# Cross-attention with sparsemax and a trigonometric FFN on one core: the context arrives transposed from the host instead of being transposed by TensorE

## What is computed

```
q = layernorm(x) @ Wq + bq;  k = ctx @ Wk + bk;  v = ctx @ Wv + bv      # 16 heads of 32
attn = sparsemax(q k^T / sqrt(32));  x = x + (attn v) @ Wo + bo
z = layernorm(x);  x = x + sqrt((z @ cos(theta+theta_noise))^2 + (z @ sin(phi+phi_noise))^2)
```

## Time and profile before

| | us |
|---|---|
| median of 3 runs | 852.85 |
| the three runs | 851.33, 852.85, 861.3 |
| the profiled execution: its span, first to last instruction (no time of its own beside it is given) | 858.3 |
| busy in it: TensorE matmul / its weight load | 681.9 / 441.6 |
| busy: VectorE / ScalarE / GpSimd | 639.5 / 480.7 / 195.8 |

### The profile page before, as it was taken

How to read it: one execution, slowest core, us unless ns; L and a number is a source line. 1 busy time by engine, 2 the same in 40 slices (tenths; PEclk the granted TensorE clock), 3 DMA queues, 4 the chain that set the end, 5 groups by cost and what they waited for, 6 DMA issues and landing times.

```text
span 858.3 us, 17053 instructions
## 1 busy us (share of the span) xinstructions
PE 681.9 (79%) x5152; PEld 441.6 (51%) x5152; DVE 639.5 (75%) x4046; ACT 480.7 (56%) x936; POOL 195.8 (23%) x147
## 2 busy tenths in 40 slices
PE   3895843879977789899889988988949898986485
PEld 3562522645555454665467455855437455742351
DVE  2799995599936997499929994799638995899401
ACT  3271754655485554875388546765537566843441
POOL 4940450001520034102520162004410053000000
PEclk9898885979989799899989999999969999998687
DMA  7620100000020000200020002000020000000000
GB/s 233 247 99 1 68 3 1 2 2 1 11 90 1 0 10 1 90 0 0 10 91 0 0 10 67 24 0 10 1 86 4 0 10 11 3 1 10 11 3 10
DMA packets 14576, 26.27 MB, mean 31 GB/s; under 512 B 2106, under 2 KB 2106, under 8 KB 14478
## 3 DMA queue, kind: packets, MB, share of 16 engines
q1 hardware_dynamic: 14478, 25.35, 8.9%
HBM read 23.71 MB, written 1.64 MB: 30 GB/s over the span
## 4 chain that ended last, share of the span: by engine, by line
DVE 71%; issue 9%; PE 7%; DMA 5%; DVEq 3%; SPq 3%; ACT 2%; ACTq 0%; POOL 0%; POOLq 0%
DVE cand L772 22%; DVE cand L784 17%; DVE top L779 14%; DMA xq<-in_x 3%; PE tps L438 3%; DVE csum L794 2%; PE work L422 2%; DMA out_y<-att 2%; DVE x L871 2%; DVE gk L797 2%; DVE topz L790 1%; DVE g_max L800 1%; SPq L197 1%; DVE st L747 1%; PE work L342 1%
## 5 line engine op out<-in xcount | busy, mean ns | idle before, releaser
L772 DVE MAX8 cand<-S 100x8 f32<-100x60 f32 (+1 forms) x1536 | 191.0, 208 | 49.0 <-ACT S L576 28.7
L438 PE MATMUL tps<-ident,S 100*128 100x100 f32 x768 | 106.0, 282 | 82.3 <-DVEq L864 47.5
L422 PE MATMUL work<-kT,qz 128*100 128x361 f16 x768 | 153.8, 342 | 0.8 <-ACT k_f L597 0.8
L613 ACT ACTIVATE S<-S,neg_tau 100x722 f32<-100x722 f32 x128 | 115.0, 900 | 68.2 <-DVE neg_tau L802 68.2
L287 POOL TENSOR_TENSOR ctxT<-ctxT_f,ctxT 128x1024 f16<-128x1024 f32 x24 | 54.0, 2248 | 426.5 <-ACT ctxT_f L576 426.5
L784 DVE MATCH_REPLACE8 cand<-top,cand 100x96 f32<-100x96 f32 x640 | 149.1, 250 | 0.0
L337 PE MATMUL work<-wv,ctxT 128*128 128x512 f16 x576 | 130.8, 384 | 19.8 <-ACT v L576 19.4
L779 DVE MAX8 top<-cand 100x8 f32<-100x96 f32 x768 | 141.2, 252 | 0.0
L438 PEld LDWEIGHTS tps<-ident,S 100*128 100x128 f32 x768 | 87.0, 158 | 104.0 <-ACT pT L576 45.5
L337 PE MATMUL work<-ctxT,wk 128*128 128x361 f16 x768 | 128.3, 329 | 10.8 <-ACT k_f L597 9.1
L576 ACT ACTIVATE S<-work 100x722 f32<-100x722 f32 x128 | 99.6, 778 | 33.0 <-PE work L422 30.8
(11 more groups left out here) (102 smaller groups left out, 671.4 us busy)
## 6 DMA issues: line engine op xcount, KB each, us to landing
ctx_nat<-in_ctx SPq DMA_DIRECT2D x8, 1280.0 KB
xq<-in_x SPq DMA_DIRECT2D x8, 200.0 KB
xr<-in_x SPq DMA_DIRECT2D x8, 200.0 KB
out_y<-att SPq DMA_DIRECT2D x8, 200.0 KB
ctx_nat<-in_ctx SPq DMA_DIRECT2D x8, 164.0 KB
wq<-in_L_xattn_Wq SPq DMA_DIRECT2D x1, 1024.0 KB, 7.4
S<-in_L_xattn_Wk SPq DMA_DIRECT2D x1, 1024.0 KB, 9.5
S<-in_L_xattn_Wv SPq DMA_DIRECT2D x1, 1024.0 KB, 11.2
```

What stands on the lines that cost most here:

```text
L422: last = nc.tensor.matmul(buf[0:L, half, 0:HALF], qz2[:, i, h // G, h % G, :], kT2[:, j, h // G, half * HALF:(half + 1) * HALF], start=(n ...
L438: last = nc.tensor.transpose(tps[:, half, c * L:(c + 1) * L], S[0:L, h, kc * P:(kc + 1) * P], ident[0:L, 0:L])
L613: nc.scalar.activation(S[0:L, h, 0:N], S[0:L, h, 0:N], ACT.Relu, bias=neg_tau[:, h:h + 1], accum_out=row_sum[:, h:h + 1]).then_inc(relu_do ...
L772: last = nc.vector.max(cand[:, j, 8 * i:8 * i + 8], S[0:L, h, cuts[i]:cuts[i + 1]])
```

## The change

The host hands the context over as (batch, 128, 4, 722), that is with the model dimension over the partitions, outside the measured time. SP loads it with one transfer straight into `ctxT_f`, now (128, 4, 722) fp32. ScalarE casts it from there to `ctxT2[:, 0]`, one instruction for each i, the third of 210 columns a chunk; GpSimd's `low_ctx` is as before but for the shorter third. `transpose_ctx` and `ctx_nat` are gone. `load_ctx(b+1)` waits for `low_ctx` of batch b. Since the ring's uses in a pass must be even, `q_of` is split in two halves on TensorE and ScalarE (28 uses instead of 30), and the semaphores that guard each slot are chosen anew. `v_of(b, 1)` starts when the slot before v0 is read, no longer when v0 is; `v_of(b, 2)` when v0 is. GpSimd zeroes the pad columns of `ctxT2` instead of the pad rows of `ctx_nat`, and the first load no longer waits for it. The diff, cut to its core:

```diff
 
-    USES = H + 1 + NC // 2 + 1 + 1 + NC // 2 + 1 + DC
+    USES = H + 1 + NC // 2 + 2 + 1 + 1 + DC
 
...
         ctxT2 = sb("ctxT2", [P, 2, DC, NC * P], F16)
-        ctxT_f = sb("ctxT_f", [P, DC, 2 * P])
+        ctxT_f = sb("ctxT_f", [P, DC, N])
         kT2 = sb("kT2", [P, 2, DC, N], F16)
...
@@ -183,12 +182,9 @@
         def _(sp):
             def load_ctx(b):
 
-                sp.wait_ge(ctx_f_ready, NC // 2 * b)
-                src = ctx_in[bass.ds(b, 1), :, :]
-                sp.dma_start(ctx_nat[:, 0:NC - 1, :],
-                             src[:, 0:(NC - 1) * P, :].rearrange("a (c p) d -> p (a c) d", p=P)).then_inc(in_ctx, 16)
-                sp.dma_start(ctx_nat[0:LAST, NC - 1, :],
-                             src[:, (NC - 1) * P:N, :].rearrange("a p d -> p (a d)")).then_inc(in_ctx, 16)
+                sp.wait_ge(ctx_lo_ready, NC // 2 * b)
+                sp.dma_start(ctxT_f[:, :, :],
+                             ctx_in[bass.ds(b, 1), :, :, :].rearrange("a p c n -> p (a c) n")).then_inc(in_ctx, 16)
 
             def load_x(buf, b, done):
                 sp.dma_start(buf[:, :], x[bass.ds(b, 1), :, :].rearrange("a l d -> l (a d)")).then_inc(done, 16)
             load_x(xq, 0, in_xq)
-            sp.wait_ge(pad_zero, 1)
-            load_ctx(0)
+            sp.dma_start(ctxT_f[:, :, :],
...
         def _(pool):
-            pool.memset(ctx_nat[64:P, NC - 1, :], 0.0).then_inc(pad_zero, 1)
+            pool.memset(ctxT2[:, :, :, N:NC * P], 0.0).then_inc(pad_zero, 1)
...
 
-                pool.wait_ge(ctx_f_ready, NC // 2 * b + i + 1)
-                at = slice(2 * i * P, 2 * (i + 1) * P)
-                pool.tensor_tensor(ctxT2[:, 1, :, at], ctxT_f[:, :, :], ctxT2[:, 0, :, at],
+                pool.wait_ge(ctx_hi_ready, NC // 2 * b + i + 1)
+                at = slice(2 * i * P, min(2 * (i + 1) * P, N))
+                pool.tensor_tensor(ctxT2[:, 1, :, at], ctxT_f[:, :, at], ctxT2[:, 0, :, at],
                                    ALU.subtract).then_inc(ctx_lo_ready, 1)
                 pool.wait_ge(ctx_lo_ready, NC // 2 * b + i + 1)
...
@@ TensorE @@
-            def q_of(b, before_v=False):
+            def q_of(b, half, sem_before, value):
...
+                pe.wait_ge(sem_before, value)
                 buf = take()
-                for m in range(DC):
+                for m in (2 * half, 2 * half + 1):
...
-            def transpose_ctx(b, i, att_before=0, v_between=True):
...
-                for j in range(2):
-                    for c in range(DC):
-                        last = nc.tensor.transpose(buf[:, j, c * P:(c + 1) * P],
-                                                   ctx_nat[:, 2 * i + j, c * P:(c + 1) * P], ident[:, :])
-                last.then_inc(work_full, 1)
...
                 if i == 0:
                     pe.wait_ge(s_ready, H * (b + 1))
+                elif i == 1 and last_pass:
+                    pe.wait_ge(att_ready, b)
+                elif i == 1:
+                    pe.wait_ge(xT_ready, b + 2)
                 else:
-                    pe.wait_ge(v_ready, NC // 2 * b + i)
-                    if last_pass:
-                        pe.wait_ge(att_ready, b)
+                    pe.wait_ge(v_ready, NC // 2 * b + i - 1)
...
                 for i in range(NC // 2):
-
                     v_of(b, i, last)
-                    if not last:
-                        transpose_ctx(b + 1, i, None if first else b)
                 if not last:
-                    q_of(b + 1)
+                    q_of(b + 1, 0, v_ready, NC // 2 * b + 2)
+                    q_of(b + 1, 1, v_ready, NC // 2 * b + 3)
...
                     else:
-                        x2T_of(b - 1, ctx_f_ready, NC // 2 * (b + 2))
-                        k_of(b + 1, 0, b)
+                        x2T_of(b - 1, q_raw_ready, 2 * (b + 1) + 1)
+                        k_of(b + 1, 0, q_raw_ready, 2 * (b + 1) + 2)
...
                     if not last:
-                        for m in range(1, DC):
-                            k_of(b + 1, m, b)
+                        k_of(b + 1, 1, k_f_ready, DC * (b + 1) + 1)
+                        k_of(b + 1, 2, sq_ready, b)
+                        k_of(b + 1, 3, k_f_ready, DC * (b + 1) + 2)
@@ ScalarE @@
-            def q_of(b):
-                copy(q_raw[:, :, :], empty()[:, 0, 0:DC * L].rearrange("p (m l) -> p m l", m=DC),
+            def q_of(b, half):
+                ms = slice(2 * half, 2 * half + 2)
+                copy(q_raw[:, ms, :], empty()[:, 0, 2 * half * L:2 * (half + 1) * L].rearrange("p (m l) -> p m l", m=2),
                      scale=SCALE).then_inc(q_raw_ready, 1)
 
             def ctxT_of(b, i):
 
-                src = empty()
-                for part, dst in ((0, ctxT2[:, 0, :, 2 * i * P:2 * (i + 1) * P]), (1, ctxT_f[:, :, :])):
-                    if part == 1 and (i > 0 or not at_start(b)):
-                        act.wait_ge(ctx_lo_ready, NC // 2 * b + i)
-                    for j in range(2):
-                        last = copy(dst[:, :, j * P:(j + 1) * P], src[:, j, :].rearrange("p (c k) -> p c k", c=DC))
-                last.then_inc(ctx_f_ready, 1)
+                if i == 0:
+                    act.wait_ge(in_ctx, 16 * (b + 1))
+                at = slice(2 * i * P, min(2 * (i + 1) * P, N))
+                copy(ctxT2[:, 0, :, at], ctxT_f[:, :, at]).then_inc(ctx_hi_ready, 1)
...
+        if name == "ctx_1024":
+            a = np.asarray(a).reshape(a.shape[0], a.shape[1], -1, P).transpose(0, 3, 2, 1)
```

More of the change, by code:

```diff
@@ L61, in build_kernel @@
     B, L, D = x.shape
-    N = ctx_in.shape[1]
+    N = ctx_in.shape[3]
     H = 16
@@ L90, in build_kernel @@
         wcos, wsin = sb("wcos", [P, DC, D]), sb("wsin", [P, DC, D])
-        ctx_nat = sb("ctx_nat", [P, NC, D])
         ctxT2 = sb("ctxT2", [P, 2, DC, NC * P], F16)
-        ctxT_f = sb("ctxT_f", [P, DC, 2 * P])
+        ctxT_f = sb("ctxT_f", [P, DC, N])
         kT2 = sb("kT2", [P, 2, DC, N], F16)
@@ L148, in build_kernel @@
         weight_step, split_ready = sem("weight_step"), sem("split_ready")
-        ctx_f_ready, k_f_ready, q_sum = sem("ctx_f_ready"), sem("k_f_ready"), sem("q_sum")
+        ctx_hi_ready, k_f_ready, q_sum = sem("ctx_hi_ready"), sem("k_f_ready"), sem("q_sum")
         ctx_lo_ready, k_lo_ready = sem("ctx_lo_ready"), sem("k_lo_ready")
@@ L356, in q_of, with k_of @@
                 last.then_inc(work_full, 1)
[L358 to L379 removed]
+            def k_of(b, m, sem_before, value):
                 if m == 0:
                     pe.wait_ge(ctx_lo_ready, NC // 2 * (b + 1))
[L384 to L389 removed]
+                pe.wait_ge(sem_before, value)
                 buf = take()
@@ L490, in _ @@
             xT_of(0, take()).then_inc(work_full, 1)
-            for i in range(NC // 2):
-                transpose_ctx(0, i, None, False)
             pe.wait_ge(in_wq, 16)
-            q_of(0, True)
+            q_of(0, 0, xT_ready, 1)
+            q_of(0, 1, xT_ready, 1)
             pe.wait_ge(split_ready, 1)
-            for m in range(DC):
-                k_of(0, m)
+            k_of(0, 0, q_raw_ready, 1)
+            k_of(0, 1, q_raw_ready, 2)
+            k_of(0, 2, k_f_ready, 1)
+            k_of(0, 3, k_f_ready, 2)
             pe.wait_ge(split_ready, 2)
@@ L523, in one_pass @@
                     v_of(b, i, last)
-                    if not last:
-                        transpose_ctx(b + 1, i, None if first else b)
                 if not last:
-                    q_of(b + 1)
+                    q_of(b + 1, 0, v_ready, NC // 2 * b + 2)
+                    q_of(b + 1, 1, v_ready, NC // 2 * b + 3)
                 if first:
-                    for m in range(DC):
-                        k_of(b + 1, m)
+                    k_of(b + 1, 0, q_raw_ready, 2 * (b + 1) + 1)
+                    k_of(b + 1, 1, q_raw_ready, 2 * (b + 1) + 2)
+                    k_of(b + 1, 2, k_f_ready, DC * (b + 1) + 1)
+                    k_of(b + 1, 3, k_f_ready, DC * (b + 1) + 2)
                     sum_flags(b, 0)
```

41 lines of the change are left out of this document (11 added, 30 removed).

## The result

| | before | after |
|---|---|---|
| median of 13 runs each, us | 854.18 | 844.62 |
| lowest and highest, us | 849.02, 861.3 | 841.15, 846.76 |
| profiled execution: span / its own time, us | 858.3 / not given | 840.8 / 843.08 |

The ratio is 0.9896, 95% interval 0.9871 to 0.992: 1.0% faster, 9.6 us between the medians. The spread of the runs fell from 12.3 to 5.6 us. The forecast was 847.0 us, within 838 to 855, and a change of under 2%.

A forecast was written before the change was run, and what follows sets the result against it. The chain was taken as 71% VectorE, with TensorE and ScalarE hardly on it. From the median of 852.85 us, 1.4 for x1 and 4.5 for the other terms gave 847.0 us, range 838 to 855.

The forecast's parts named there:

- The removed work, 0: Context transposes and evictions under the third threshold group: about 29 us of ScalarE and 26 of TensorE, counted as nothing directly.
- The x1 add: VectorE's add, freed from GpSimd's third `low_ctx`: 7.9 us of the profiled execution, 1.4 (two thirds of one meeting) in ordinary runs.
- The third `low_ctx` against topz, 0: Third threshold group's end: GpSimd done at 405.2, 0.4 us before topz; cost 0, bounds 0 and 1.77 us a pass.
- Rival 1: Slower: third `low_ctx` lands on topz to neg_tau, up to 1.77 us in each of six passes, 857.6 us; chance 0.12.
- The start, 2.5: DMA queue at 8 to 12 us, slowed by the 82-partition context transfer: 2.5 us gained, bounds 0 and 3.2.
- `angles`, 1.2: Start, beside GpSimd: two VectorE instructions lose their doubling, 0.6 us each, 1.2 us; bounds 0 and 6.2.
- Batch 0's groups, 0.8: End of batch 0's threshold groups: half of 1.6 us stretching of topz and csum beside GpSimd goes; bounds -1.8 and 1.6.
- The entries, taken as unchanged: Store of y to MAX8 between batches: none of these steps is edited, so no gain was counted.
- a stretch other than 14.3 us: Sign that the forecast is wrong: store to MAX8 (435.75 to 450.09) no longer 14.3 us.
- Rival 3: TensorE's relief shortens re-entry into a pass: a third of 6.3 us in seven passes, 832.3 us; chance 0.05.
- Other edits, 0: q's eviction as two of about 0.33 us, changed waits and memset: cost 0, bounds 0 and 5 us for q.
- Rival 2: No change: early DMA gap is from bias transfers and stays, no x1 meetings in ordinary runs; 851.6 us, chance 0.15.

The follow-up runs named there:

- a_dummies: Changed kernel with 24 unused fp32 transposes on TensorE and ten unused casts on ScalarE in each first and middle pass: 845.08 us, ratio 0.987.
- a_v_serial: Changed kernel with `v_of(b, 1)` and `v_of(b, 2)` again waiting for the eviction of the v before them: 854.46 us, ratio 0.9989.
- b_low_after_x1: Kernel before, with the third `low_ctx` of the middle passes held back until the x1 add is done: 846.83 us, ratio 0.9914.
- b_start96: Kernel before, first context load without the wait for `pad_zero` and its last block as 96 partitions instead of 82: 852.93 us, ratio 0.998.
- b_split80: Kernel before, with the context's last block loaded as 80 and 2 partitions instead of 82: 853.44 us, ratio 0.9999.
- a_rows4: Changed kernel with the first context load cut into four transfers of 2,888-byte rows: 843.65 us, ratio 0.987.
- a_fill: Changed kernel with 18 unused filler matmuls on TensorE in each middle-pass entry: 843.03 us, ratio 0.9853.
- a_best: Changed kernel with two VectorE instructions of `settle` merged into one and 18 filler matmuls in each middle entry: 836.76 us, ratio 0.9773.
- b_again: Kernel before, unchanged, run for a second profile: 854.2 us, ratio 1.0009.
- a_again: Changed kernel, unchanged, run for a second profile: 843.85 us, ratio 0.9859.

## Why the prediction was right, and where not

**The removed work, 0: right.** a_dummies puts more than the ScalarE work and 16.9 of TensorE's 24.0 us back for 0.5 to 1.2 us, within noise; a_v_serial leaves it out and gains nothing; b_low_after_x1 keeps it and gains 7.7. In busy time TensorE's 24.0 us is just under the 25 to 30 that I had named as a sign, and the 17.5 us of span are more than half of either engine's.

**The x1 add: mechanism and place right, the term for ordinary runs too small.** 7.9 us of the profiled execution is what went. But "two thirds of one meeting", 1.4 us, was read out of two medians a few microseconds apart. Four profiles of the unmended order show 4, 3, 3 and 2 meetings, so 4 to 8 us; b_low_after_x1 measured 7.7. This is the larger part of what makes 9.6 us out of 5.9. A tie within some 10 ns falls either way in each of six passes, 12 of 24 here, and its mean should have been taken as three meetings, 5.9 us. That the forecast lies within 2.4 us of the measured median all the same is in part luck: from 854.18, the median of before over thirteen runs, the same terms give 848.3.

**The third `low_ctx` against topz, 0: right,** with a margin of 0.62 us in the pass shown where 0.4 was worked out, and a start 4.31 us ahead of x1 where it was 4.1 (407.58 - 403.5). In the second middle pass the margin is 0.09 us, so the 0 was near. Rival 1 did not happen, and a_v_serial shows that it was real: 3.1 us later and the meeting falls on gk.

**The start, 2.5: cause right, too small.** Measured 3.4, over the upper bound of 3.2. Giving the last block of the old layout 96 partitions brings 2.9 of it (b_start96), cutting 2 partitions off it 1.1 (b_split80). The wait for `pad_zero`, counted at 0, is 0.07 us. The step that failed is the length of the stretch: I took the loss to end at 12 us, but from 12 to 14 us the kernel before moved 124 GB/s, and the changed one 406. The 1.46 MB more that the changed kernel moves from 8 to 14 us are 3.7 us at 390 GB/s, and wq lands 3.5 us earlier. Row length is no part of it (a_rows4).

**`angles`, 1.2: the size right, the working not.** 35.2 us from bn_stats to MAX8 became 34.1. But two instructions lost 1.23 us each while the two that were to lose 0.6 each gained as much; that the sum came out at 1.1 is luck. **Batch 0's groups, 0.8:** 0.65 measured, of a stretch that takes 50.8 to 53.0 us over the profiles here. I had counted two stretched instructions and left out gk at 102.09 (0.83 us) and 120.23 (1.24) and neg_tau at 103.34 (0.31); and meetings moved rather than went, topz at 113.88 now taking 1.45 us. The timeline of the changed kernel:

```profile
96.18 0.62 DVE L761 TENSOR_TENSOR topz<-top 100x192 f32<-100x192 f32 x1
...
113.88 1.45 DVE L761 TENSOR_TENSOR topz<-top 100x192 f32<-100x192 f32 x1
```

**The entries, taken as unchanged: wrong in the profile, open in the median.** I named a stretch other than 14.3 us as a sign against me, and it was 12.95. Rival 3 had this outcome by another cause: fewer matmuls. The runs show another cause: TensorE's granted clock, which in single executions of either kernel is 0.50 to 0.67 in some entries (7.4 to 8.6 us from bn_stats to MAX8, with two at 8.95 and 9.22 where `ln_sd` was late too) and 0.84 to 1.00 in others (6.3 to 7.0). a_fill, with more matmuls, held it at 1.00. Two cases stand apart at a clock of 1.00: a_best, with its late `ln_sd`, and one entry of b_split80 at 8.21 us, in which the scores were there 2.64 us before MAX8 and VectorE's stretch behind `settle` was longer, for a reason that its chain does not show:

```profile
442.77 4.54 issue
```

The means over the entries of batches 3 to 6 are 8.11, 7.50, 7.87 and 7.53 us in the four profiles of the unmended order (before, b_again, b_split80, b_start96), 6.71 in b_low_after_x1, and 6.75, 7.23, 7.73 and 7.36 in the changed kernel and the variants that keep its entries (after, a_again, a_rows4, a_dummies). The two sets overlap. Whether the change shifts the odds, at some 0.5 us an entry, stays open.

**Not foreseen: the flag that meets `low_k`,** 1.37 us in two of the profiles. Whether the change makes it likelier is open (two of six against none of five). It is a meeting of the kind that I had priced elsewhere and did not look for here.

**Other edits, 0:** q's two evictions take 322 ns each, as worked out, and no stretch of VectorE waits on them. **Rival 2,** that start and x1 give nothing in ordinary runs, fell with b_low_after_x1 and the 3.4 us of the start; b_start96 keeps the bias loads and fills the queue all the same (DMA share 1.03 from 8 to 10 us).

**The sum.** 5.9 us were predicted, 9.6 measured. With three meetings for two thirds of one (+4.5) and 3.4 for 2.5 (+0.9) the forecast would have been 852.85 - 11.3 = 841.6, 3 us under the measured median. Part of that is the median of before, which was 852.85 in the three runs I started from and 854.18 in thirteen; against its own before the measured gain of 9.6 is 1.7 us under 11.3, and the runs don't say which term is too large.

## What to carry to other kernels

When two engines reach a shared SBUF port within a few tens of nanoseconds, take one profile's count of meetings as one throw: price the mean over executions, and look at the spread of the runs, which fell from 12.3 to 5.6 us with this change and to 6.5 with the one wait of b_low_after_x1. Moving the off-path instruction by a wait or an order gives most of what removing its producer gives, so try the placement first; and when an engine is relieved, work out where its successor lands, since a_v_serial took all the gain back by landing 3 us elsewhere. Before crediting a wait to the engine named, look when that engine was done: 34 of the 56 entries here ended with VectorE's own stretch, not with the scores.
